# Moving half of the identity adds to GpSimd, and one bias in four from TensorE to VectorE

## The reference

```python
# step 1: attention pooling with a mask by the sequence's type (prefix, postfix, all but itself)
scores = tanh(x @ W1 + b1) @ v                       # [64, 128]
p = softmax(where(mask, scores[:, None, :], -1e30))  # [64, 128, 128]
x = x + (p @ x) / mask.sum(-1, keepdims=True)
# step 2: a linear layer chosen by category, 512 x 512, 64 categories
x = x + (x @ W[cat] + b[cat])
```

## Time and profile before

| | us |
|---|---|
| median of 3 runs | 314.0 |
| the profiled execution's own time | 313.81 |
| its span in the profile | 311.7 |
| PE busy | 304.5 (98%) |
| DVE busy | 285.6 (92%) |
| ACT busy | 275.5 (88%) |
| POOL busy | 47.9 (15%) |
| DMA q1, share of 16 engines | 84.2% |

### The profile page before, as it was taken

One profiled execution on the slowest core, in us unless ns is written; L12 is line 12 of the kernel. 1 busy time (PEld: TensorE's weight loads), 2 busy tenths in 40 slices (PEclk: granted clock), 3 DMA queues, 4 the chain that ended last, 5 costly groups with the idle time before them and its releaser, 6 DMA issues.

```text
span 311.7 us, 4825 instructions
## 1 busy us (share of the span) xinstructions
PE 304.5 (98%) x1308; PEld 236.7 (76%) x1308; DVE 285.6 (92%) x397; ACT 275.5 (88%) x447; POOL 47.9 (15%) x93
## 2 busy tenths in 40 slices
PE   7999999999999999999999999999999999999995
PEld 4444786778788787878888788787878878887884
DVE  4459999999999999999999999999999999999960
ACT  2387997999999899998999999899999989999953
POOL 5010302204040130403003040210404012000000
PEclk9999999999999999999999999999999999999999
DMA  7999999998979899798989989799898989965123
GB/s 274 362 424 380 416 418 401 327 419 255 412 280 373 326 316 424 266 402 300 353 361 293 412 282 394 289 361 392 266 410 298 374 313 329 416 242 195 52 84 135
DMA packets 21213, 101.51 MB, mean 326 GB/s; under 512 B 2369, under 2 KB 2370, under 8 KB 11074
## 3 DMA queue, kind: packets, MB, share of 16 engines
q1 hardware_dynamic: 20898, 99.89, 84.2%
q10 hardware_dynamic: 288, 1.31, 1.1%
HBM read 84.41 MB, written 16.78 MB: 325 GB/s over the span
## 4 chain that ended last, share of the span: by engine, by line
PE 88%; DMA 6%; DVE 2%; ACT 1%; issue 1%; ACTq 0%; SPq 0%
PE ps_y L593 17%; PE ps_y L591 17%; PE ps_y L592 17%; PE ps_pre L553 12%; DMA w_raw<-in_L_cond_W 6%; PE ps_y L606 5%; PE ps_y L603 4%; PE ps_y L604 4%; PE ps_y L605 4%; PE ps_pT L570 2%; PE ps_scores L563 2%; PE ps_y L579 1%; PE ps_scores L561 1%; DVE w_lo L409 1%; ACT probs L302 1%
## 5 line engine op out<-in xcount | busy, mean ns | idle before, releaser
L409 DVE TENSOR_TENSOR w_lo<-w_raw,w_hi 128x2048 fp32r<-128x2048 f32 x60 | 137.4, 2289 | 0.9 <-ACT w_hi L280 0.9
L280 ACT ACTIVATE w_hi<-w_raw 128x2048 fp32r<-128x2048 f32 x60 | 114.8, 1913 | 10.8 <-DVE w_raw L397 10.7
L591 PE MATMUL ps_y<-w_hi,xT_hi 128*128 128x512 f32 x240 | 95.0, 396 | 0.0
L593 PE MATMUL ps_y<-w_hi,xT_lo 128*128 128x512 f32 x240 | 93.8, 391 | 0.0
L592 PE MATMUL ps_y<-w_lo,xT_hi 128*128 128x512 f32 x240 | 93.6, 390 | 0.0
L593 PEld LDWEIGHTS ps_y<-w_hi,xT_lo 128*128 128x128 f32 x240 | 45.1, 188 | 9.8
L592 PEld LDWEIGHTS ps_y<-w_lo,xT_hi 128*128 128x128 f32 x240 | 45.1, 188 | 9.4
L591 PEld LDWEIGHTS ps_y<-w_hi,xT_hi 128*128 128x128 f32 x240 | 45.1, 188 | 8.5
L437 DVE TENSOR_TENSOR z_lo<-ps_y,z_hi 128x512 fp32r<-128x512 f32 x64 | 43.7, 685 | 5.0 <-ACT z_hi L316 5.0
L397 DVE TENSOR_TENSOR w_raw<-w_raw,ident 128x512 f32<-128x512 f32 x63 | 43.1, 684 | 4.8 <-DMA w_raw<-in_L_cond_W 4.8
L231 POOL COPY mask<-penalty 128x128 bf16 x64 | 42.5, 686 | 14.1 <-issue 14.1
(11 more groups left out here) (68 smaller groups left out, 328.1 us busy)
## 6 DMA issues: line engine op xcount, KB each, us to landing
w_raw<-in_L_cond_W SPq DMA_DIRECT2D x63, 1024.0 KB, 7.5
out<-out_sb SPq DMA_DIRECT2D x64, 256.0 KB, 5.1
x_raw<-in_x SPq DMA_DIRECT2D x15, 1024.0 KB, 5.5
x_raw<-in_x SPq DMA_DIRECT2D x2, 512.0 KB, 4.7
w_raw<-in_L_cond_W ACTq DMA_DIRECT2D x1, 1024.0 KB, 6.3
w_pack<-in_W_b_v ACTq DMA_DIRECT2D x1, 257.0 KB, 2.7
b_raw<-in_L_cond_b SPq DMA_DIRECT2D x2, 128.0 KB, 12.7
ids_row<-in_ids SPq DMA_DIRECT2D x1, 0.5 KB
```

Source lines behind the costliest of these rows:

```text
L280: nc.scalar.activation(w_hi[k % NH][:], w_raw[k % NW][:], ACT.Copy).then_inc(w_hi_ready, 1)
L409: nc.vector.tensor_tensor(w_lo[k % NL][:], w_raw[k % NW][:], w_hi[k % NH][:].bitcast(F32), ALU.subtract).then_inc(w_lo_ready, 1)
L591: nc.tensor.matmul(y[:], xT_hi[q][:, c, xs], w_hi[k % NH][:, c, :], start=(c == 0), stop=False)
L593: last = nc.tensor.matmul(y[:], xT_lo[q][:, c, xs], w_hi[k % NH][:, c, :], start=False, stop=(c == DC - 1))
```

## The change

GpSimd takes over the identity of W for k % 4 = 1 and 2 from k = 5 on, 30 of 64. For each it waits until VectorE has finished a given instruction: w_lo of k - 2 for k % 4 = 1, av_lo of the group for k % 4 = 2.

For k % 4 = 1 (16 sequences, called wide) TensorE no longer adds the bias. SyncE spreads the row of 512 biases over 128 partitions by a DMA into `out_sb[1]`, ahead of need (`load_wide`), and VectorE adds the PSUM bank to it there (`add_wide`) in place of ScalarE's copy. Store and reuse of the bank wait for the new semaphore `sum_ready` in these cases.

```diff
+    WIDE = 1
         def wi_count(k):
-            return {3: 6, 4: 5}.get(k, k + 2)
+            return {3: 6, 4: 5}.get(k, k + 2 - pool_count(k - 1))
+        def by_pool(k):
+            return k > G and k % G in (1, 2)
+        def pool_count(k):
+            return max(k // G - 1, 0) * 2 + (min(k % G, 2) if k > G else 0)
+        def wide(k):
+            return k % G == WIDE
+        def wait_out(engine, k):
+            if wide(k):
+                engine.wait_ge(sum_ready, k // G + 1)
+            else:
+                engine.wait_ge(out_ready, k - (k + G - WIDE - 1) // G + 1)
...                                                     # SyncE
             def store(k):
-                sp.wait_ge(out_ready, k + 1)
+                wait_out(sp, k)
+            def load_wide(g):
+                cat = sp.value_load(ids_row[0:1, G * g + WIDE:G * g + WIDE + 1], min_val=0, max_val=C - 1)
+                if g >= 1:
+                    sp.wait_ge(out_stored[WIDE], 16 * g)
+                sp.dma_start(out_sb[WIDE][:], bias[bass.ds(cat, 1), :].to_broadcast([P, D])).then_inc(wide_in, 16)
             load_w(6)
+            load_wide(0)
...
                 if b == 3 and g + 3 < GROUPS:
                     load_x(g + 3)
+                if b == 2 and 1 <= g < GROUPS:
+                    load_wide(g)
                 if t + 2 + NW < B:
                     load_w(t + 2 + NW)
...                                                     # GpSimd
+            def add_identity(k):
+                pool.wait_ge(w_in[k % NW], 16 * (k // NW + 1))
+                if k % G == 1 and k - 2 > G:
+                    pool.wait_ge(w_lo_ready, w_count(k - 2))
+                elif k % G == 2 and k - 2 > G:
+                    pool.wait_ge(av_lo_ready, k // G + 1)
+                blocks = w_raw[k % NW][:].rearrange("p c (i j) -> p (c i) j", j=P)[:, ::DC + 1, :]
+                eye = ident[:].rearrange("p (a j) -> p a j", a=1).to_broadcast([P, DC, P])
+                nc.gpsimd.tensor_tensor(blocks, blocks, eye, ALU.add).then_inc(pool_wi_ready, 1)
             for g in range(GROUPS):
+                if g >= 1:
+                    add_identity(G * g + 1)
+                    add_identity(G * g + 2)
                 pool.wait_ge(exp_ready, g + 1)
...                                                     # ScalarE
             def split_w_hi(k):
-                act.wait_ge(wi_ready, wi_count(k))
+                if by_pool(k):
+                    act.wait_ge(pool_wi_ready, pool_count(k))
+                else:
+                    act.wait_ge(wi_ready, wi_count(k))
...
-            copy_out(1)
...
-                copy_out(k - 3)
                 if b == 0 and g + 1 < GROUPS:
                     split_xT_hi(g + 1)
+                if not wide(k - 3):
+                    copy_out(k - 3)
...                                                     # VectorE
+            def add_wide(g):
+                k = G * g + WIDE
+                dve.wait_ge(pz_done, k + 1)
+                dve.wait_ge(wide_in, 16 * (g + 1))
+                nc.vector.tensor_tensor(out_sb[WIDE][:], ps_y[k % NY][:], out_sb[WIDE][:], ALU.add)\
+                    .then_inc(sum_ready, 1)
...
-            add_identity(5)
...
-            add_identity(6)
...
             add_identity(7)
+            add_wide(0)
...
-            add_identity(9)
...
-            add_identity(10)
...
                 split_z_lo(k - 1)
-                if k + 4 < B:
+                if b == 0:
+                    add_wide(g - 1)
+                if k + 4 < B and not by_pool(k + 4):
                     add_identity(k + 4)
...                                                     # TensorE
             def xw(k):
                 if k >= NY:
-                    pe.wait_ge(out_ready, k - NY + 1)
+                    wait_out(pe, k - NY)
...                                                     # in pz
-                nc.tensor.matmul(y[:], mh, z_lo[k % NZ][:], start=False, stop=False, skip_group_check=True)
+                last = nc.tensor.matmul(y[:], mh, z_lo[k % NZ][:], start=False, stop=wide(k), skip_group_check=True)
+                if wide(k):
+                    last.then_inc(pz_done, 1)
+                    return
                 nc.tensor.matmul(y[:], one_hot[:, k:k + 1].to_broadcast([P, P]), b_both[:],
                                  start=False, stop=True, skip_group_check=True).then_inc(pz_done, 1)
```

More of the change, by code:

```diff
@@ L44, in program @@
     NX, NT, NW, NH, NL, NZ, NO, NY = 3, 2, 5, 4, 3, 3, 4, 5
+    WIDE = 1
+    assert NO == G
     RAW = G
@@ L138, in program @@
         wi_ready = sem("wi_ready")
+        pool_wi_ready = sem("pool_wi_ready")
         w_hi_ready = sem("w_hi_ready")
@@ L161, in program @@
         out_ready = sem("out_ready")
+        sum_ready = sem("sum_ready")
+        wide_in = sem("wide_in")
         block = ctx.enter_context(nc.Block())
@@ L170, in wi_count @@
         def wi_count(k):
-            return {3: 6, 4: 5}.get(k, k + 2)
+            return {3: 6, 4: 5}.get(k, k + 2 - pool_count(k - 1))
[3 more added lines that the diff above has]
+            return max(k // G - 1, 0) * 2 + (min(k % G, 2) if k > G else 0)
+        assert all(pool_count(k) == sum(by_pool(i) for i in range(k + 1)) for k in range(B))
+        def wide(k):
[5 more added lines that the diff above has]
+                engine.wait_ge(out_ready, k - (k + G - WIDE - 1) // G + 1)
         @block.sync
```

## The result

The changed kernel takes 311.06 to 311.16 us (medians of two sets of 6 runs) against 314.5 to 315.2 in the same sets: ratio 0.9886 (95% interval 0.9853 to 0.9919), and 0.9912 (0.9878 to 0.9946) when measured again. The profiled execution took 310.89 us, span 308.9. The forecast was 307.9 with a range of 306.0 to 313.0. The direction came out and the time lies in the range, but the size did not come out, and what sets the pace after the change was forecast wrong. In profiled executions the change gives 2.9 us, forecast were 6.1.

A forecast was written before the change was run, and what follows sets the result against it. It took VectorE and ScalarE to lead in a near tie, TensorE 0.19 us behind; bias matmuls -3.4, scores wait -2.5, group 2 -0.5, lead-in +0.3 made -6.1 from 313.8, 307.7, plus 0.2 for the median: 307.9 us, range 306.0 to 313.0.

The forecast's parts named there:

- VectorE leads the kernel before: Steady groups: VectorE and ScalarE set the 18.44 us pace by a hair, TensorE having 0.19 us in hand.
- the wait at the scores: TensorE's second scores matmul waits for VectorE's av_lo; losing 0.19 us of waiting in 13 groups was to save 2.5 us.
- the forecast 18.25: TensorE's own work per group in the kernel before, without its waits for VectorE: 18.25 us.
- 15 bias matmuls at 0.228 us: TensorE: bias matmuls removed from its path, 0.228 us each by starts, 3.4 us in all.
- GpSimd's add at 1.2 us, its hold on VectorE 0.2 us per group: Each identity add takes GpSimd 1.2 us; the first of a group delays VectorE's next w_lo by 0.2 us.
- the mask copy of the earlier trace: GpSimd copy, normally 0.29 us, took 1.97 us beginning inside VectorE's xT_lo; read as VectorE holding GpSimd.
- VectorE then needs 17.7 us, still under 18.02.: Per group after the change: VectorE's work including GpSimd's hold is 17.7 us, TensorE's 18.02, forecast as the cadence.
- nothing is lost: GpSimd's second add of a group, after av_lo, ends at 159.61, before VectorE's next w_lo at 159.78.
- The lead-in at +0.3 and group 2 at -0.5 us: Lead-in costs +0.3 us (-0.85 to +1.1) from GpSimd delaying divisor; group 2's 0.80 us transpose wait gives 0.5 us back.
- DMA: Spread bias adds 0.7 us per group to the DMA engines, 16.8 becoming 17.5 us, under 18.02, so it hides.
- Only the matmuls count: Rival, chance 0.27: GpSimd's adds take back VectorE's room; groups take 18.2 to 18.4 us, time 310 to 313 us.
- The two slow ones: Rivals: long GpSimd add holding VectorE, about 336 us, chance 0.08; dear spreading over partitions, about 345 us, chance 0.05.

The follow-up runs named there:

- e1: Changed kernel with only GpSimd's 30 identity adds; all bias back on TensorE, copies on ScalarE: 312.73 us, ratio 0.9936 to the kernel before.
- e15: e10 with a fifth output buffer, two for the spread bias, so each spread is issued a group ahead: 308.98 us, ratio 0.9821 to the kernel before.
- e9: Changed kernel with VectorE's identity add moved ahead of w_lo in steps with b = 3: 311.7 us, ratio 0.9894 to the kernel before.
- e8: Changed kernel with GpSimd's adds cut to 8 elements instead of 512, same order and waits: 308.27 us, ratio 0.9781 to the kernel before.
- e5: Changed kernel with the first bias add moved behind the identity of W 8 on VectorE: 312.71 us, ratio 0.9889 to the kernel before.
- e6: Changed kernel with GpSimd's adds starting at W 13, earlier ones staying on VectorE: 310.85 us, ratio 0.9864 to the kernel before.
- e7: Changed kernel with the edits of e5 and e6 together: 311.06 us, ratio 0.9865 to the kernel before.
- e4: Changed kernel without the 15 spreads after the first: 311.57 us, ratio 0.9908 to the kernel before.
- e10: Changed kernel with the spread bias for k % 4 = 3 instead of 1, its add between z_lo and the maximum: 316.11 us, ratio 1.0025 to the kernel before.

## Why the prediction was right or wrong

**VectorE leads the kernel before, and the wait at the scores goes.** Right, shown by the changed kernel and by e1, whose 18.22 is the forecast 18.25.

**15 bias matmuls at 0.228 us.** Right as the price of TensorE's own work (18.22 in e1, 17.98 in e15). In the changed kernel TensorE did not set the pace, so less than this and the wait at the scores together came out: 0.32 us per group, not 0.42.

**GpSimd's add at 1.2 us, its hold on VectorE 0.2 us per group.** Right in size: 1.29, and the w_lo beside the first add is 2.47 us long instead of 2.28; the second add held nothing. But by e9 and e15, where this hold stays and the cadence is 17.98 or 17.99, it cost the changed kernel nothing. The rule that I took from the Trainium skill (SBUF — State Buffer, § Who interferes with whom), that the hold goes both ways, agrees with this 0.19 us and with e8, where it is gone; the mask copy of the earlier trace rows had shown the other way.

**"VectorE then needs 17.7 us, still under 18.02."** The step that failed in the steady part. The sum of each engine's work was right and the conclusion from it wrong: the pace was not the larger of the two sums but a loop that crosses from one engine to the other. I counted the bias add at 0.60 us of VectorE's room and didn't ask what stands behind it in VectorE's list: xT_lo, for which TensorE's hidden layer waits. The bias add's 0.60 us and the divisor's 0.17 both lie on that loop. Together they make it 0.11 us per group longer than the forecast 18.02, 1.2 us in the part compared above; take away either (0.17 in e9, 0.60 in e15) and TensorE's 17.98 is back. The sentence "nothing is lost" for the second add missed the divisor in the same way: it stands on GpSimd, was held by VectorE's identity add from 0.20 to 0.41 us, and cost the loop 0.17. It starts no later than before, 4.5 us behind the second scores matmul; but VectorE, with an identity add less ahead, starts the next one after 4.20 us, not 4.82, and so beside it.

**The lead-in at +0.3 and group 2 at -0.5 us.** The larger miss, 2.2 us, and beyond the +1.1 that was given as the lead-in's upper bound. The first part was right: GpSimd's add of W 6 was held by a w_lo, and the reciprocal came at 34.24 (forecast 34.1, before 33.81):

```profile
32.32 1.73 POOL L274 TENSOR_TENSOR w_raw<-w_raw,ident 128x512 f32<-128x512 f32 x1 [4.57 <-DMA w_raw<-in_L_cond_W]
34.02 0.19 POOL L316 TENSOR_TENSOR row_div<-row_sum,seen 128x4 f32<-128x4 f32 x1
```

I let the delay end there. In the timelines of the changed kernel it grows at three places (the line at 55.99 is the transposes of group 2):

```profile
42.42 1.92 ACT L336 ACTIVATE w_hi<-w_raw 128x2048 fp32r<-128x2048 f32 x1 [1.16 <-DVE w_raw L453]
47.10 3.07 DVE L465 TENSOR_TENSOR w_lo<-w_raw,w_hi 128x2048 fp32r<-128x2048 f32 x1
55.99 0.66 PE L632 MATMUL ps_pT<-ident,probs 128*128 128x128 f32 x4 [0.80 <-ACT probs L358]
60.93 0.47 PE L615 MATMUL ps_pre<-xT_hi,w_hi 128*128 128x512 f32 x1 [0.62 <-issue]
```

ScalarE waits for the identity of W 8, which stands behind the first bias add, and the tanh comes a microsecond late. GpSimd starts the add of W 10 at 46.72, just ahead of a w_lo, and holds it for 0.79 us. Then xT_lo ends at 60.83 and the hidden layer starts 1.0 us behind the matmul ahead of it, where it was 0.72 before the change (at 59.33). The step that failed is this term of the sum: the forecast followed GpSimd's delay to the first reciprocal and no further, and did not put the bias add of the lead-in on ScalarE's path to the tanh at all. Measured from group 1 to group 3, the bias add's place is worth about 0.9 us (e5) and GpSimd's early adds 0.6 to 0.7 (e6), 1.5 together (e7). With short adds nothing is lost, the bias add in its place or not (e8, 65.60 and 37.97 us), so the two are not independent. The 0.5 us at group 2 did not return: the transposes still wait 0.80 us there, in the changed kernel as before.

**DMA.** 0.91 x 18.44 + 0.7 was forecast as 17.5 us; 0.98 x 18.13 is 17.8, so a spread costs about 1.0 us of the engines, not 0.7; e4, at 0.92 x 18.13 = 16.7, says 1.1. It hid, by e4. Whether the one W that came late in e9 was late by the spread is not shown.

**The rivals.** "Only the matmuls count" gave 310 to 313 and came nearest to the time, 311, with the right remark that lists ordered by hand keep their waits, but for a wrong reason: the add was not 1.45 us or more, and a group takes 18.13 us, not 18.2 to 18.4. That the time lies in this case's 310 to 313 is luck: without the 2.2 us that the lead-in missed it would be about 309. The two slow ones did not come.

## What to carry to other kernels

With engines within 3% of each other, a sum of work per engine is only a lower bound. Before costing a moved instruction at nothing, follow the list behind it to the next instruction that another engine waits for, and close the loop back to the start: its length is the cadence. Do the same for the lead-in, which has a list of its own. And a new operation belongs where its engine waits already (e15), with its operand loaded a whole round ahead (e10 against e15).

## What the runs showed of the hardware

GpSimd and VectorE hold each other in both directions, and longer the more they overlap: a GpSimd add of 1.29 us that has 0.32 or 0.92 us to go when a w_lo starts makes it 2.47 or 3.07 us long instead of 2.28; a 128 x 4 multiply on GpSimd takes 0.20 us alone and 0.41 when it begins inside VectorE's identity add. A spread of one 2 KB row over 128 partitions lands after 5.7 us at the median in a queue where stores of the same size took 6.2, so by its landing a row read 128 times is not dearer than a store. By the engines' time, 1.0 us against the 0.7 that 256 KB take at the mean rate, it is.
